# A graph layer kernel on one core: the edges' one-hot products in 64x64 quadrants, two slots at a time, and two operands of the attention read from PSUM by VectorE

## What is computed

```python
xn = layernorm(x)
# gnn: weighted sum over the edges into a node, then two dense layers
agg = segment_sum(edge_val[:, None] * xn[src], dst, N)
g = relu(((1 + eps) * xn + agg) @ W1.T + b1) @ W2.T + b2
# mix: hyperbolic maps around a 768-wide projection with batchnorm and a linear attention over 8 groups
x = x + g + mix(xn)
# ffn: 1024 hidden units with gelu, kept only for the top half of the nodes by a routing weight
x = x + ffn(layernorm(x))
```

## Time and profile before

| | |
|---|---|
| median of 3 runs | 2598.59 us (2598.03 to 2598.87) |
| the profiled execution | 2601.07 us, its span 2599.4 us |
| busy in the span | PE 95%, DVE 69%, POOL 68%, ACT 56% |

### The profile page before, as it was taken

How to read it: one execution, slowest core, us unless ns; L and a number is a source line. 1 busy time by engine, 2 the same in 40 slices (tenths; PEclk the granted TensorE clock), 3 DMA queues, 4 the chain that set the end, 5 groups by cost and what they waited for, 6 DMA issues and landing times.

```text
span 2599.4 us, 42294 instructions
## 1 busy us (share of the span) xinstructions
PE 2475.5 (95%) x12654; PEld 2169.1 (83%) x12654; DVE 1804.0 (69%) x5986; ACT 1461.6 (56%) x3513; POOL 1769.9 (68%) x1879
## 2 busy tenths in 40 slices
PE   4898999999999999999999999999999999999996
PEld 3677888887888888888888888888788888888786
DVE  6847676676766768667667776675866767767557
ACT  3755565565655656556565565665655656556431
POOL 2037777777777777777777777777777777777500
PEclk9899999999999999999999999999999999999998
DMA  7643444434444344443444434444344343343338
GB/s 231 189 132 107 128 115 120 125 114 129 115 121 126 114 120 123 121 124 116 120 125 116 130 115 120 124 117 128 113 120 123 115 130 116 115 124 114 97 117 282
DMA packets 192007, 333.45 MB, mean 128 GB/s; under 512 B 46287, under 2 KB 133965, under 8 KB 191673
## 3 DMA queue, kind: packets, MB, share of 16 engines
q0 software_dynamic: 86752, 238.17, 32.0%
q1 hardware_dynamic: 105018, 92.42, 11.1%
HBM read 291.99 MB, written 38.46 MB: 127 GB/s over the span
## 4 chain that ended last, share of the span: by engine, by line
PE 78%; DVE 9%; DMA 5%; ACT 5%; issue 1%; SPq 0%; POOL 0%; DVEq 0%; POOLq 0%
PE bank L1157 23%; PE qkv L1252 13%; PE bank L1264 12%; PE bank L1171 9%; PE bank L1201 6%; DMA work<-in_x 5%; PE qkv L1181 4%; PE bank L498 2%; PE qkv L1180 2%; DVE rings L960 2%; PE bank L1217 2%; PE bank L1226 2%; PE bank L1191 2%; ACT work L796 1%; ACT work L799 1%
## 5 line engine op out<-in xcount | busy, mean ns | idle before, releaser
L766 POOL DMA_INDIRECT rings<-xn_dram,window x1764 | 1744.0, 989 | 615.9 <-issue 388.4
L1157 PE MATMUL bank<-rings 128*128 128x256 f32 x3528 | 885.3, 381 | 17.9 <-DVE rings L960 14.3
L1157 PEld LDWEIGHTS bank<-rings 128*128 128x128 f32 x3528 | 657.4, 191 | 111.1 <-DVE rings L960 25.6
L960 DVE TENSOR_SCALAR rings<-iota,window_dst,window 128x128 f32<-128x128 f32 x1764 | 559.9, 363 | 139.2 <-PE bank L1157 125.6
L1252 PE MATMUL qkv<-work,ffn_weights 128*128 128x256 f32 x1568 | 365.4, 381 | 0.0
L1264 PE MATMUL bank<-ffn_weights,work 128*128 128x256 f32 x1568 | 362.0, 379 | 0.0
L856 ACT ACTIVATE work<-qkv,fb 128x256 f32<-128x256 f32 x392 | 159.8, 472 | 312.8 <-PE qkv L1252 312.3
L1264 PEld LDWEIGHTS bank<-ffn_weights,work 128*128 128x128 f32 x1568 | 297.2, 190 | 40.0
L1252 PEld LDWEIGHTS qkv<-work,ffn_weights 128*128 128x128 f32 x1568 | 295.7, 191 | 38.5
L1171 PE MATMUL bank<-resident,weights 128*128 128x256 f32 x1176 | 277.8, 379 | 0.0
L1171 PEld LDWEIGHTS bank<-resident,weights 128*128 128x128 f32 x1176 | 223.3, 190 | 30.3
(11 more groups left out here) (240 smaller groups left out, 3364.6 us busy)
## 6 DMA issues: line engine op xcount, KB each, us to landing
rings<-xn_dram,window POOLq DMA_INDIRECT x1764, 2.8
xn_dram<-work SPq DMA_DIRECT2D x14, 896.0 KB, 7.7
work<-xn_dram SPq DMA_DIRECT2D x49, 256.0 KB
work<-in_x SPq DMA_DIRECT2D x48, 256.0 KB
out<-work SPq DMA_DIRECT2D x48, 256.0 KB
work<-in_x SPq DMA_DIRECT2D x9, 896.0 KB, 5.7
rings<-out SPq DMA_DIRECT2D x6, 896.0 KB, 8.6
out<-rings SPq DMA_DIRECT2D x6, 896.0 KB, 6.3
```

Source lines behind the costliest of these rows:

```text
L766: nc.gpsimd.indirect_dma_start(out=msg[q][:, :], out_offset=None, in_=xn_dram[:, :], in_offset=bass.IndirectOffsetOnAxis(ap=window[t % WIN ...
L960: v.tensor_scalar(sel[k % SEL_RING], iota[:, :], window_dst[b][:, k % SLOTS:k % SLOTS + 1], window[b][:, k % SLOTS, 2:3].bitcast(F32), ALU ...
L1157: te.matmul(agg[h][:, 0:D], sel[k % SEL_RING], msg[q], start=first, stop=last, skip_group_check=True).then_inc(slot_used, 1)
```

## The change

**Edges.** A tile's edges are now split by the half of 64 nodes they go into. Each half has its own start in the edge list, and a slot holds 64 edges of one half in partitions 0 to 63 and 64 of the other in partitions 64 to 127; odd and even slots swap the halves. So `sel` is 128 x 64, and a slot is two products with 64 rows, 64 columns of weights and 256 columns of data, each in its own quadrant of the array (`tile_position`). Two successive slots together name all four quadrants. Even slots add up in one bank and odd ones in the other, for both tiles, and `take_sup` adds the two banks with one more VectorE instruction per tile. TensorE issues edges in bursts of 6 slots instead of singly, and the tables `PE_AT` and `DVE_AT` are rewritten. A half tile has room for 18 x 64 = 1,152 edges; what is over goes through `rem_chunk` in chunks of 64 per half. A window takes four DMAs instead of one. The table part of the head has four border gathers instead of two and a new part, `tables_halves`, after group 3.

**Attention.** `mix_v` no longer copies v and writes relu(q); VectorE reads both from PSUM in `mix_ratio`, which then frees `qkv`.

```diff
-SEL_RING = 12
+SEL_RING = 18
+HALF = 64
+BURST = 6
-    WIN = SLOTS * P
+    PAIRS = SLOTS // 2
+    WIN = SLOTS * HALF
...
+        def tables_halves(dve):
...
+            link(v.tensor_scalar(tmp_p[:NT], ends_bc[:NT, 0, :], thr_half[:NT, 0:1], BIG, ALU.is_lt, ALU.mult))
+            link(v.tensor_tensor(tmp_p[:NT], tmp_p[:NT], iota_m[:NT], ALU.add))
+            v.tensor_reduce(lohi[:NT, 1:2], tmp_p[:NT], AX_X, ALU.min)
...
-            for k in range(2):
+            for k in range(4):
                 nc.gpsimd.indirect_dma_start(
                     out=border[k][:NT].bitcast(I32), out_offset=None, in_=dst.rearrange("(r j) -> r j", j=P),
...
-        PE_AT = dict(sup=0, x3=0, qkv=(0, 10), w1=1, h1=(12, 17, 20), w2=4, outT=(13, 23), ft=(16, 27), hid=(23, 23,
+        PE_AT = dict(sup=0, x3=0, qkv=(0, 12), w1=3, h1=(12, 17, 21), w2=4, outT=(13, 26), ft=(18, 32), hid=(24, 26,
...
             def rem_chunk(t):
                 counted(pool, rem_used, rem)
-                at_ = pool.snap(rem_at, min_val=0, max_val=3 * E)
-                pool.dma_start(rem_edges[:, :], edges[bass.ds(at_, 3 * P)].rearrange("(p n) -> p n", p=P)
-                               ).then_inc(rem_edges_landed, 16)
+                for u in range(2):
+                    at_ = pool.snap(rem_at[u], min_val=0, max_val=3 * (ET * P + WIN))
+                    pool.dma_start(rem_edges[HALF * u:HALF * (u + 1), :],
+                                   edges[bass.ds(at_, 3 * HALF)].rearrange("(p n) -> p n", p=HALF)
+                                   ).then_inc(rem_edges_landed, 16)
...
-                s.activation(v_raw, v_in, ACT.Copy)
-                s.activation(rk, k_in, ACT.Relu)
-                s.activation(rq, q_in, ACT.Relu).then_inc(v_read, 1)
+                s.activation(rk, k_in, ACT.Relu).then_inc(k_read, 1)
...
-                v.tensor_scalar(sel[k % SEL_RING], iota[:, :], window_dst[b][:, k % SLOTS:k % SLOTS + 1],
+                v.tensor_scalar(sel[k % SEL_RING], at_half[k % 2], window_dst[b][:, c:c + 1],
...
-                dve.wait_ge(v_read, i * 2 + (h + 1))
-                link(v.scalar_tensor_tensor(v_raw, v_raw, s_col[h], om, ALU.mult, ALU.mult))
-                link(v.scalar_tensor_tensor(v_raw, vs, 2.0, v_raw, ALU.subtract, ALU.mult))
+                dve.wait_ge(k_read, i * 2 + (h + 1))
+                link(v.scalar_tensor_tensor(v_raw, role_in(2), s_col[h], om, ALU.mult, ALU.mult))
+                v.scalar_tensor_tensor(v_raw, role_in(0), 0.0, v_raw, ALU.max, ALU.mult).then_inc(v_read, 1)
...
-                v.scalar_tensor_tensor(sup[h], xnin[h], eps1_col, agg[h][:, 0:D], ALU.mult, ALU.add
-                                       ).then_inc(sup_ready, 1)
+                link(v.scalar_tensor_tensor(sup[h], xnin[h], eps1_col, agg[0][:, h * D:(h + 1) * D], ALU.mult, ALU.add))
+                v.tensor_tensor(sup[h], sup[h], agg[1][:, h * D:(h + 1) * D], ALU.add).then_inc(sup_ready, 1)
...
+            def quadrants(h, n, one_hot, rows_, start, stop):
+                for r in range(2):
+                    u = n ^ r
+                    ins = te.matmul(agg[n][HALF * u:HALF * (u + 1), h * D:(h + 1) * D], one_hot[HALF * r:HALF * (r + 1)],
+                                    rows_[HALF * r:HALF * (r + 1)], start=start, stop=stop, skip_group_check=True,
+                                    tile_position=(HALF * r, HALF * u))
+                return ins
...
-                te.matmul(agg[h][:, 0:D], sel[k % SEL_RING], msg[q], start=first, stop=last,
-                          skip_group_check=True).then_inc(slot_used, 1)
+                    ins = quadrants(h, k % 2, sel[k % SEL_RING], msg[q], start, stop)
+                    if k % 2:
+                        ins.then_inc(slot_used, 2)
```

More of the change, by code:

```diff
@@ L113, in build @@
         work = sb("work", [P, 11120])
+        window_dst = [work[:, 7424 + SLOTS * b:7424 + SLOTS * (b + 1)] for b in range(WINDOWS)]
         def view(base, at, *shape):
@@ new lines, in tables_borders @@
+            for k in range(3):
+                v.tensor_copy(border_f[k][:NT], border[k][:NT].bitcast(I32))
+            link(v.tensor_copy(border_f[3][:NT], border[3][:NT].bitcast(I32)))
+            v.tensor_scalar(border_t[0][:NT], border_f[0][:NT], thr[:NT], BIG, ALU.is_lt, ALU.mult)
+            v.tensor_scalar(border_t[1][:NT], border_f[1][:NT], thr_half[:NT, 0:1], BIG, ALU.is_lt, ALU.mult)
+            v.tensor_scalar(border_t[2][:NT], border_f[2][:NT], thr_half[:NT, 1:2], None, ALU.is_le)
@@ new lines, in tables_borders @@
+            link(v.tensor_scalar(border_t[3][:NT], border_f[3][:NT], lohi[:NT, 8:9], None, ALU.is_le))
+            for k in range(2):
+                v.tensor_tensor(border_t[k][:NT], border_t[k][:NT], iota[:NT, :], ALU.add)
+            v.scalar_tensor_tensor(border_t[2][:NT], iota[:NT, :], 1.0, border_t[2][:NT], ALU.add, ALU.mult)
+            link(v.scalar_tensor_tensor(border_t[3][:NT], iota[:NT, :], 1.0, border_t[3][:NT], ALU.add, ALU.mult))
+            for k in range(3):
+                v.tensor_reduce(lohi[:NT, 4 + k:5 + k], border_t[k][:NT], AX_X, ALU.min if k < 2 else ALU.max)
@@ L431, in norm_vector @@
                     tables_chunks(dve)
+                if g == 3:
+                    tables_halves(dve)
                 if g == 4:
@@ L709, in load_window, with column @@
         def load_window(eng, t):
-            first = eng.value_load(bounds[0:1, 2 * t:2 * t + 1], min_val=0, max_val=ET * P)
-            after(eng, slot_used, RING + (t - WINDOWS + 1) * SLOTS)
-            eng.dma_start(window[t % WINDOWS][:, :, :].rearrange("p k c -> p (k c)"),
-                          edges[bass.ds(first * 3, 3 * WIN)].rearrange("(p n) -> p n", p=P)
-                          ).then_inc(window_landed[t % WINDOWS], 16)
+            flat_window = window[t % WINDOWS][:, :, :].rearrange("p k c -> p (k c)")
+            for u in range(2):
+                first = eng.value_load(bounds[0:1, 3 * t + u:3 * t + u + 1], min_val=0, max_val=ET * P)
+                if u == 0:
+                    after(eng, slot_used, RING + (t - WINDOWS + 1) * SLOTS)
+                for n in range(2):
+                    r = u ^ n
+                    eng.dma_start(flat_window[HALF * r:HALF * (r + 1), 3 * PAIRS * n:3 * PAIRS * (n + 1)],
+                                  edges[bass.ds((first + HALF * PAIRS * n) * 3, 3 * HALF * PAIRS)].rearrange("(p n) -> p n", p=HALF)
+                                  ).then_inc(window_landed[t % WINDOWS], 16)
+        def column(k):
+            return (k % 2) * PAIRS + k // 2
         def main_sync(sp):
@@ L794, in mix_v @@
                 after(act, om_ready, i * 2 + h)
-                q_in, k_in, v_in = (qkv[:, role].rearrange("p i s c -> p (i s c)") for role in range(3))
+                k_in, v_in = role_in(1), role_in(2)
                 link(s.activation(om, v_in, ACT.Square, scale=s_col[h], bias=att_eps_col))
@@ L1270, in step @@
                 for k in range(STEP_SLOTS):
[L1271 to L1272 removed]
+                    if k % BURST == BURST - 1 and (i > 0 or k >= EARLY_EDGES):
+                        edges_of(i, k - (BURST - 1))
                     if j >= 0:
@@ L1302, in main_tensor @@
             bn_products(pe)
+            bn_moments(pe)
             mix_h1(0, 0)
             mix_h1(0, 1)
-            bn_moments(pe)
-            for k in range(EARLY_EDGES):
-                edge(0, k)
+            for k in range(0, EARLY_EDGES, BURST):
+                edges_of(0, k)
             pe.wait_ge(bn_ready, 1)
-            te.matmul(agg[1][:, 0:1], ident[:, :], ident[:, 0:1], start=True, stop=True).then_inc(rem_used, 1)
+            te.matmul(banks[2][:, 20:21], ident[:, :], ident[:, 0:1], start=True, stop=True).then_inc(rem_used, 1)
             mix_h1(0, 2)
```

170 lines of the change are left out of this document (94 added, 76 removed).

## The result

The changed kernel takes 2747.3 us (2742.0 to 2757.2), the kernel before, on the same chip, 2598.3 us (2595.4 to 2598.9): ratio 1.057, with a 95% interval of 1.0553 to 1.0588. I had forecast 2623 us and a range up to 2725 us. It is slower, as forecast, but by six times as much, outside the range.

A forecast was written before the change was run, and what follows sets the result against it. GpSimd, without slack, and TensorE were taken to bound the loop together. From 2601.07 us, +15 head, +36 remainders, -20 slow gathers, -11 edge products, +4 loop start gave 2625.1, less 2.5: 2623 us; range 2575 to 2725 us.

The forecast's parts named there:

- Costed at nothing: ScalarE's relief, VectorE's extra add, three more window DMAs per tile and later release of `qkv`: no cost.
- GpSimd's slow gathers: Gathers beside VectorE's long two-SBUF-input instructions; one input of two of them moves to PSUM: -20 us (0 to -50).
- Edge products: TensorE's edge products: four quadrants at once, 7.8 us a step, switches 1.9; only the lag at the end gained, -11 us.
- Quadrants keep the old pace: Rival on TensorE: a pair of slots takes as long as before, switches are added; 2711 us, chance 0.22.
- Head: Table building before the loop: more instructions in `tables_halves` and `tables_borders`, two more border gathers, nothing hidden: +15 us (13 to 17).
- Remainders: Six extra chunks, all on GpSimd, which has no slack: 6.0 us each, +36 us (27 to 54).
- Start of the loop: Step 0: slots 12 to 17 come as one late burst, `qkv` freed later, GpSimd stalls: +4 us (0 to 8).
- The signs of the profile: Profile after: same 0.30 us gaps, mean gather about 0.978 us, TensorE busy some 300 us less, gather waits 5 us a step.

The follow-up runs named there:

- x_at_3: The changed kernel with one number of VectorE's table as before (x=3 for x=0): 2642.9 us, ratio 1.0167 to the kernel before.
- x_loaded_first: The changed kernel with x=0 kept, but SyncE loads x ahead of xn: 2649.4 us, ratio 1.018 to the kernel before.
- before_x_at_0: The kernel before with x=0 for x=3 and nothing else: 2673.8 us, ratio 1.0274.
- edges_x_at_0: The changed kernel (x=0) with the attention of before: 3472.9 us on a chip where the kernel before takes 2994.7 us, ratio 1.158.
- diagonal_third: x_at_3 with odd slots sent into the same two quadrants as even ones, two at a time instead of four: 2767.2 us, ratio 1.0649 to the kernel before.
- no_remainder: x_at_3 with the remainder chunks left out (edges past a half tile's 1,152 dropped): 2622.4 us, 20.6 us less than x_at_3.

## Why the prediction was wrong

**The step that failed is "Costed at nothing".** Its parts were the relief of ScalarE, VectorE's add, the window DMAs and the later release of `qkv`, and it never priced what the change section shows: that `DVE_AT` and `PE_AT` are rewritten. One of those numbers, x from 3 to 0, is 104 of the 149 us. The trace of before had what was needed: VectorE waits there 141.0 us in 48 waits, 2.9 us each, for this very load, at a place from which no wait reaches GpSimd (4 us of ring waits in all).

```profile
DVE work L1023 <- DMA work<-in_x: 141.0, 48, 4.6
```

Moved three rows earlier, ahead of `mix_n4`, the same wait becomes 211.3 us and has ScalarE, TensorE and GpSimd behind it. x_at_3 shows the cost, x_loaded_first that it is the load, before_x_at_0 that it needs nothing else of the change.

**In the same step, the later release of `qkv`** was costed at nothing as "covered by a burst of edges". Alone on the kernel before it costs 160 us. In the changed kernel the wait is there as well (93.8 us, and 101.9 us in x_at_3). In x_at_3 it is nearly hidden: GpSimd has 3.1 us of ring waits in all, so next to nothing that TensorE waits for reaches it. The quadrants pay for the attention part: with them TensorE is busy for 41.8 of 46.6 us in the mean of all steps, and this wait takes 2 of the 4.8 us left. How much of the 104 us would go away without the attention part is open; edges_x_at_0 was meant to tell and ran on one of the chips where it can't.

**"GpSimd's slow gathers", -20 us: wrong.** The mean gather went from 0.989 to 0.991 us, not to 0.978. With the attention part alone it is 0.981 us, 14 us in all, but that loop is slower and VectorE less busy in it (65% for 70%), so this is not shown to come from the operands. I counted, for every gather of over 1.0 us, what it has above the median of 0.946 us, and put it to the VectorE instruction that it overlaps most: 73.4 us before, 74.5 after, 58.7 with attention alone. After the change the first moved instruction (L1027), with its input in PSUM, has 12.6 us beside it, where L979 had 2.5 before. Most of what the edges part takes back stands beside the one-hot matrices (L1008): 15.8 us, with attention alone 5.4. This is overlap, not cause.

**"Edge products", right.** All four quadrants work at once. The eight MATMULs of two slots start in two groups of four, a group within 0.02 us, and there is a group every 0.216 us; before, one MATMUL started every 0.216 us. So a slot takes 0.216 us, the 0.217 that I took, and what is above it in the 0.242 us is the switches. Going into a burst and out of it delays the MATMULs around it too: from the last start before the burst shown to the second start behind it are 2.085 us (the median of 113 such bursts), where 8 x 0.216 = 1.73 would be the bare rate. That is 0.36 us a burst, 0.18 a switch; I had taken 0.19. In x_at_3 TensorE is busy for 42.7 us in the step with FFN shown above, forecast 41.5. The time behind the last gather fell by 6.3 us (10.0 in x_at_3), forecast 11.

The rival "Quadrants keep the old pace" is refuted for this kernel: where they do keep it, in diagonal_third, the time is 121 us above. It had taken its force from the Trainium skill, "TensorE: Matmul & The Clock Gate", Part 3, by which matmuls start strictly in program order. The trace agrees with that order: the four starts lie 0.006 to 0.007 us behind each other. It doesn't agree with what I drew from it, that four products behind each other can't overlap: 24 MATMULs take 1.45 us. The order is not the one that I assumed, either: the wait for a second slot's data stands at the third weight load of each eight, by which I read that the first MATMULs of four products go ahead of their second ones. And it was my misreading, for the same Part says that matmuls in different tiles of the array run concurrently. "TensorEngine Tiling (Array Packing)" of the Trainium skill, Tiling Modes, says that tiles work in parallel, and the trace agrees, with these 1.45 us beside the 2.74 us of two quadrants.

**"Head", +15 us: right**, 14.4. TensorE is fed later there; compare the second row, where it was busy for all of 20 us:

```profile
100.00:120.00 20.00, 10.17 (x49) 8.64 (x50) 19.00 (x99) 11.39 (x63) 1.20 (x2) 0.74 0.40 116
```

**"Remainders", +36 us: right where they stand**, 34 us in the changed kernel; but without them x_at_3 is only 20.6 us faster. One chunk on GpSimd in order of time, between two gathers:

```profile
941.37 1.15 POOL L789 DMA_DIRECT2D rem_edges<-in_edges  x2
944.54 1.18 POOL L795 DMA_INDIRECT rem_msg<-xn_dram,rem_edges  x1 [2.01 <-DMA rem_edges<-in_edges]
945.80 0.24 POOL L798 TENSOR_SCALAR rem_dst<-rem_edges 128x1 f32<-128x1 int32 x1
946.23 0.81 POOL L801 TENSOR_SCALAR rem_sel<-rings,rem_dst,rem_edges 128x128 f32<-128x128 f32 x1 [0.20 <-POOL rem_dst L798]
947.21 1.06 POOL L811 DMA_INDIRECT rings<-xn_dram,window  x1 [0.17 <-issue]
```

From this chunk's start to the next gather are 5.84 us, of which 0.3 us would be there anyway; the mean of the six is 5.7 us against 6.0.

**"Start of the loop", +4 us: right in size** for the first step, which has 2.9 us of ring waits (before 1.3); they are part of the 102.6 us.

**The signs of the profile.** Forecast were a fall of TensorE's busy time by some 300 us and waits for gathers of 5 us a step. It fell by 148 us (166 in x_at_3), and there are 1.2 us of such waits in all (20.5 in x_at_3). TensorE's room went into waits for ScalarE and VectorE and into a lower granted clock behind them (0.96 in the loop, before 1.00), which lengthens the MATMULs. With x_at_3 the forecast's own terms hold: +13.8 head, +35.3 loop, -10.0 end, 39.1 us in all against the 44 of the sum without the -20. That is luck in part: no_remainder's loop is still 11.9 us above before, so the loop's excess is not the chunks alone. No kernel of this study is faster than the kernel before on a usual chip: the engine that sets the pace, GpSimd, got 34 us more to do and its start 14 us later, and nothing less.

## What to carry to other kernels

When a change rewrites a table that places instructions, price each number that moved: look in the trace of before for what that instruction waits for, and ask what is queued behind it at its new place. A wait that no other engine feels at one row can stop four engines three rows earlier. And a part that looks like relief ("ScalarE copies less") must be read by who now frees the buffer, above all where the engine that waits for it is at 100%.

## What was not expected of the hardware

- Four 64x64 quadrants of TensorE run float32 products at once: 24 MATMULs of 256 columns in 1.45 us; two at once take 2.74 us. Between products of the whole array, such a burst costs 0.36 us more than its bare rate of 0.216 us a slot.
- After a wait of 2.3 us (attention alone) or 4.65 us (the changed kernel) TensorE comes back at half its clock (granted 0.50), so the price was well above the wait: eight MATMULs in 3.78 us instead of 1.89, and 3.8 us a step for a wait of 2.3. After 1.19 us, in x_at_3, eight take 1.99 us at a granted clock of 1.00.
- The same kernel takes 2600 us on some chips and 3000 us on others, with the same duration of gathers and activations, longer waits between engines and a lower granted clock; and the order of kernels differs between them.
